# Second attention of a vision block: a gathering matmul for two units at once, and heads' rows stored dense on 68 partitions

## The reference, cut to what matters

```python
    def _L0_ffn_ref(x, Wq, bq, Wk, bk, Wv, bv, Wr, br, Wo, bo):
        ...
        dist = jax.nn.softmax(jnp.mean(x @ Wr + br, axis=1), axis=-1)
        _, idx = jax.lax.top_k(dist, N_ACTIVE)
        idx = jnp.sort(idx, axis=-1)
        ...
        Qs, Ks, Vs = (gather(Q), gather(K), gather(V))
        scale = 1.0 / jnp.sqrt(jnp.asarray(D_ATTN, x.dtype))
        score = jax.nn.softmax(jnp.einsum('bhqd,bhkd->bhqk', Qs, Ks) * scale, axis=-1)
        O = jnp.einsum('bhqk,bhkd->bhqd', score, Vs)
        O = O.transpose(0, 2, 1, 3).reshape(b, s, N_ACTIVE * D_ATTN)
        return O @ Wo + bo
    h = _L0_tok_ref(x, L0_tok_W, L0_tok_b, L0_tok_pos_emb)
    h = jnp.concatenate([jnp.broadcast_to(cls_tok, (h.shape[0], 1, h.shape[2])), h], axis=1)
    h = h + _L0_attn_ref(_layernorm(h, axis=-1), ...)
    h = h + _L0_ffn_ref(_layernorm(h, axis=-1), ...)
```

## Time and profile before

| what | value |
|---|---|
| device time, three runs | 388.31, 391.5, 392.24 us; median 391.5 |
| the profiled execution | 390.81 us, of which 389.0 us from its first to its last instruction (span) |
| busy share of the span | PE 81%, PEld 65%, DVE 66%, ACT 52%, POOL 44% |
| mean clock granted to PE | 0.851 of full |
| first weight transfer of the loop issued, last one issued | 224.8 us, 335.2 us |
| last stores of heads' rows issued | from 353.5 us |

### The profile page before, as it was taken

The page is one execution under the profiler, slowest core; times in us unless marked ns, Lnnn a source line. Parts: engine busy times, 40 slices in busy tenths (PEclk is TensorE's granted clock), DMA queues, the critical chain, the costliest instruction groups (busy, mean ns, idle before and its releaser), DMA issues.

```text
span 389.0 us, 14942 instructions
## 1 busy us (share of the span) xinstructions
PE 314.6 (81%) x6334; PEld 253.9 (65%) x6334; DVE 257.0 (66%) x546; ACT 203.2 (52%) x463; POOL 169.3 (44%) x193
## 2 busy tenths in 40 slices
PE   1999999888977888785897468998889698585787
PEld 0897768535855565554795258888789687483366
DVE  2355446455578888887696776797878678462365
ACT  1023323465877777742488037777777566352320
POOL 4755000004266666642055074576657656563200
PEclk9999999999975555555698559999999999679989
DMA  7997810003500000000000068999998899824714
GB/s 206 373 424 246 248 79 0 0 0 127 199 4 5 4 3 6 3 5 3 3 2 1 0 211 266 287 289 288 258 284 272 241 286 276 249 51 97 229 54 178
DMA packets 52275, 55.97 MB, mean 144 GB/s; under 512 B 25296, under 2 KB 49008, under 8 KB 51696
## 3 DMA queue, kind: packets, MB, share of 16 engines
q1 hardware_dynamic: 51632, 52.78, 43.1%
q0 software_dynamic: 576, 2.23, 1.8%
HBM read 45.04 MB, written 9.96 MB: 141 GB/s over the span
## 4 chain that ended last, share of the span: by engine, by line
PE 37%; SPq 23%; DVE 14%; issue 10%; DMA 6%; ACT 6%; POOL 4%; POOLq 0%; ACTq 0%; DVEq 0%
SPq L457 21%; PE ps L1366 11%; PE ps L1389 5%; PE ps L1520 4%; POOL r L527 4%; DVE r L1022 4%; PE ps L1727 3%; PE ps L1449 2%; DVE rs L1032 2%; PE ps L1404 2%; PE ps L1471 2%; DVE mx L1007 2%; DMA ring<-wsplit 2%; DMA r<-in_x 2%; DMA r<-padded_rows,idx 2%
## 5 line engine op out<-in xcount | busy, mean ns | idle before, releaser
L520 POOL TENSOR_TENSOR r<-r,cst 128x1088 f32<-128x1088 f32 x16 | 33.0, 2062 | 61.6 <-DVE ring L958 58.7
L1366 PE MATMUL ps<-r 128*128 128x256 f32 x192 | 45.8, 395 | 8.6 <-DMA r<-in_x 8.6
L1366 PEld LDWEIGHTS ps<-r 128*128 128x128 f32 x192 | 37.7, 199 | 15.6 <-issue 10.5
L805 ACT ACTIVATE r<-ps 128x504 f16<-128x504 f32 (+1 forms) x50 | 31.9, 664 | 27.9 <-PE ps L1571 27.5
L1594 PE MATMUL ps<-r,ring 128*128 128x68 f16 x840 | 34.6, 201 | 12.2 <-DMA ring<-wsplit 11.3
L1471 PE MATMUL ps<-r 17*32 17x34 f32 x2048 | 30.5, 242 | 16.1 <-DVE r L1022 11.2
L1471 PEld LDWEIGHTS ps<-r 17*32 17x32 f32 x2048 | 27.3, 142 | 24.1 <-DVE r L1022 18.3
L1594 PEld LDWEIGHTS ps<-r,ring 128*128 128x128 f16 x840 | 32.1, 101 | 16.5 <-DMA ring<-wsplit 13.2
L733 ACT ACTIVATE r<-r,cst 128x136 f32<-128x136 f32 x128 | 39.9, 401 | 0.0
L609 POOL TENSOR_TENSOR r<-r,quad 128x476 f16<-128x476 f16 x38 | 37.4, 1010 | 0.6
L527 POOL TENSOR_TENSOR r<-r,rinv 128x544 f32<-128x544 f32 x16 | 18.3, 1142 | 35.3 <-DVE rinv L1036 35.3
(11 more groups left out here) (170 smaller groups left out, 696.2 us busy)
## 6 DMA issues: line engine op xcount, KB each, us to landing
ring<-wsplit SPq DMA_DIRECT2D x140, 192.0 KB, 3.3
r<-in_x SPq DMA_DIRECT2D x3, 1536.0 KB, 15.9
padded_rows<-r SPq DMA_DIRECT2D x9, 448.0 KB, 5.2
r<-in_w SPq DMA_DIRECT2D x4, 768.0 KB, 7.5
wsplit<-ring SPq DMA_DIRECT2D x1, 3072.0 KB, 11.6
r<-in_x SPq DMA_DIRECT2D x4, 384.0 KB, 8.9
h<-in_pos SPq DMA_DIRECT2D x1, 1536.0 KB, 12.1
out<-h SPq DMA_DIRECT2D x3, 512.0 KB, 2.9
```

The source lines that it names most:

```text
L520: pool.tensor_tensor(free(kx[:, u % 2, 0, :], (ROWH, UI), (NTOK, HH), (1, NTOK)), free(kr[:, 0, UI * NTOK * u:], (NTOK, UI), (0, HH), (1, ...
L1366: mm = pe.matmul(bank((n - 1) % 2, 0, D), xT[:, c, k, i * P:(i + 1) * P], tokw[:, k, :], start=k == 0, stop=k == PKT - 1)
```

## The change

It does four things in the second attention.

1. A gathering matmul has 112 moving columns, for two units. xg becomes two buffers, each for a pair of units: `xg_even` at the old place and `xg_odd` in the allocation r1. A pair of units takes 17 fills of 4 matmuls: 16 of 4 tokens of one k, and one with the last token of all four k. 17 fills stand before unit 0; units 0 to 7 gather for the pair of units that comes two later, 9 fills in even and 8 in odd units; unit 8 gathers nothing.
2. The block-diagonal matrices have a pitch of 17 columns a pair, 68 in all, so weigh2 writes 68 partitions, and o2 is stored from 68 partitions, 14 pieces of 256 B each, dense, into `pair_rows`.
3. The values get a 65th column of ones (zeros in the low half), so weigh2 also gives the sum of the exponentials. `total` and `inverse` leave; `head_out` takes a reciprocal of 7 sums from the bank before each multiplication.
4. The pair table is made in three pieces: units 0 and 1, units 2 and 3 (behind the drains of the first 17 fills), the rest in unit 1.

```diff
-PITCH = QROW * HD2
+PITCH = NTOK * HD2
+VCOL = HD2 + 2
...
-            return bass.AP(padded_rows.tensor, (v * PU + IPG * lo) * PITCH, [(HD2, P), (IPG * PITCH, n), (1, HD2)])
+            return bass.AP(pair_rows.tensor, (v * PU + IPG * lo) * PITCH, [(HD2, TCOL), (IPG * PITCH, n), (1, HD2)])
...
-        NFILL = 8
-        FILL_ACT = [0, 2, 4, 6, 7]
-        FILL_DVE = [1, 3, 5]
...
+        NFILL = 17
+        SLOT_ON_ACT = (True, False, True, False, True, False, True, True)
+        EXTRA = 1
+        FILLS = []
+        for u in range(0, NV, 2):
+            FILLS += [(u, 2, (k,), first, 4) for k in range(2 * KT) for first in range(0, NTOK - 1, 4)]
+            FILLS += [(u, 2, tuple(range(2 * KT)), NTOK - 1, 1)]
+        ON_ACT = [at % 3 != 1 for at in range(NFILL)]
+        IN_SLOT = {}
+        for v in range(NV - 2):
+            for f, on_act in enumerate(SLOT_ON_ACT):
+                IN_SLOT[v, f] = [len(ON_ACT)]
+                ON_ACT.append(on_act)
+                if f == EXTRA and v % 2 == 0:
+                    IN_SLOT[v, f].append(len(ON_ACT))
+                    ON_ACT.append(True)
...
             def store_rows(v):
                 sp.wait_ge(o2_ready, 2 * (v + 1))
-                sp.dma_start(rows_of(v), o2[:, v % 2]).then_inc(o2_stored[v % 2], 16)
+                sp.dma_start(rows_of(v), o2[0:TCOL, v % 2]).then_inc(o2_stored[v % 2], 16)
...
-            for u in range(2):
-                pool.memset(free(bd[:, u, 0, 0, NTOK:], *gaps), 0.0).then_inc(bd_clear, 1)
+            for x in range(2):
+                pool.memset(free(v2[:, 0, x, 0, HD2:], (2 * GU * VCOL, 2), (VCOL, GU), (1, 1)), 1.0 - x).then_inc(ones_set, 1)
...
+                if v == 0:
+                    clear_odd_gaps(0)
+                    clear_odd_gaps(KT)
...
-                pool.indirect_dma_start(og[:, s, :], None, padded_rows,
+                pool.indirect_dma_start(og[:, s, :], None, pair_rows,
...
+            def head_out(v, r):
+                at = 2 * v + r
+                dve.wait_ge(pv2_done, at + 1)
...
+                dve.reciprocal(rinv[0:TCOL, r, 0:GR], free(bank(weigh_bank(v, r), HD2)[0:TCOL], (VCOL, GR)))\
+                    .then_inc(rinv2_ready, 1)
+                dve.wait_ge(rinv2_ready, at + 1)
+                dve.tensor_tensor(o2[0:TCOL, v % 2, GR * r:GR * r + GR, :],
+                                  free(bank(weigh_bank(v, r))[0:TCOL], (VCOL, GR), (1, HD2)),
+                                  free(rinv[0:TCOL, r, :], (1, GR), (0, HD2)), ALU.mult).then_inc(o2_ready, 1)
...
+            def gather_fill(at):
+                u, units, ks, first, tokens = FILLS[at]
+                if u in (2, 4) and begins_unit(at, ON_ACT[at]):
+                    pe.wait_ge(pairs_ready, u // 2 + 1)
...
+                cols = PU * units
+                for i, (k, n) in enumerate((k, first + n) for k in ks for n in range(tokens)):
                     x = (xh, xl)[k // KT]
                     lo = P * (k % KT)
-                    mm = pe.matmul(bank(fill_bank(at), PU * i, PU * i + PU), x[:, n, lo:lo + P],
-                                   pairs_of[:, PU * v:PU * v + PU], start=True, stop=True)
+                    mm = pe.matmul(bank(fill_bank(at), cols * i, cols * i + cols), x[:, n, lo:lo + P],
+                                   pairs_of[:, PU * u:PU * u + cols], start=True, stop=True)
...
-                        mm = pe.matmul(bank(weigh_bank(v, r), HD2 * i, HD2 * i + HD2), bd[:, v % 2, b, g, :], v2[:, v % 2, x, g, :],
-                                       start=m == 0, stop=m == 2)
+                        mm = pe.matmul(bank(weigh_bank(v, r), VCOL * i, VCOL * i + HD2 + 1)[0:TCOL], bd_of(v)[:, b, g, :],
+                                       v2[:, v % 2, x, g, 0:HD2 + 1], start=m == 0, stop=m == 2)
```

More of the change, by code:

```diff
@@ L218, in build @@
         bo_ready = sem("bo_ready")
[L219 removed]
+        ones_set = sem("ones_set")
         picked = sem("picked")
@@ L374, in build, with fills_until, filled_by, begins_unit @@
         OG_FIRST = 4
[L375 to L381 removed]
+        NFILL = 17
[14 more added lines that the diff above has]
+                    ON_ACT.append(True)
+        assert len(ON_ACT) == len(FILLS)
+        def fills_until(at, on_act):
+            return sum(e == on_act for e in ON_ACT[:at])
+        def filled_by(v):
+            return 1 + max(at for at, (u, n, *_) in enumerate(FILLS) if u <= v < u + n)
+        def begins_unit(at, on_act):
+            return at == min(i for i in range(len(FILLS)) if FILLS[i][0] == FILLS[at][0] and ON_ACT[i] == on_act)
+        def fill_ends(at):
+            u, units, ks, first, n = FILLS[at]
+            if len(ks) > 1:
+                return (free(xg_of(u)[:, 0, first:], (2 * PU * QROW, len(ks)), (QROW, PU * units)),
+                        free(bank(fill_bank(at)), (PU * units, len(ks)), (1, PU * units)))
+            return (free(xg_of(u)[:, ks[0], first:], (QROW, PU * units), (1, n)),
+                    free(bank(fill_bank(at)), (1, PU * units), (PU * units, n)))
         block = ctx.enter_context(nc.Block())
@@ L796, in _, with fill_out, fills_out @@
             act.wait_ge(wo1_done, NTOK)
-            def fill_out(v, f):
-                at = NFILL * v + f
+            def fill_out(at):
+                u = FILLS[at][0]
                 act.wait_ge(fill_done, at + 1)
-                if v >= 2 and f == 0:
-                    act.wait_ge(v2_in, 2 * (v - 1))
-                    act.wait_ge(qk_done, 2 * (v - 1))
-                first, n = fill_tokens(f)
-                nc.scalar.activation(free(xg[:, v % 2, f // 2, first:], (QROW, PU), (1, n)),
-                                     free(bank(fill_bank(at)), (1, PU), (PU, n)), ACT.Copy).then_inc(fill_act, 1)
+                if u >= 4 and begins_unit(at, True):
+                    act.wait_ge(v2_in, 2 * (u - 2))
+                    act.wait_ge(qk_done, 2 * (u - 2))
+                dst, src = fill_ends(at)
+                nc.scalar.activation(dst, src, ACT.Copy).then_inc(fill_act, 1)
+            def fills_out(v, *slots):
+                for f in slots:
+                    for at in IN_SLOT.get((v, f), ()):
+                        if ON_ACT[at]:
+                            fill_out(at)
             def q_out(v, r):
@@ L1185, in _, with fill_out, fills_out @@
             one_hot(0, 2 * PU)
-            def fill_out(v, f):
-                at = NFILL * v + f
+            def fill_out(at):
+                u = FILLS[at][0]
                 dve.wait_ge(fill_done, at + 1)
-                if v >= 2 and f == 1:
-                    dve.wait_ge(v2_in, 2 * (v - 1))
-                    dve.wait_ge(qk_done, 2 * (v - 1))
-                first, n = fill_tokens(f)
-                dve.tensor_copy(free(xg[:, v % 2, f // 2, first:], (QROW, PU), (1, n)),
-                                free(bank(fill_bank(at)), (1, PU), (PU, n))).then_inc(fill_dve, 1)
+                if u >= 4 and begins_unit(at, False):
+                    dve.wait_ge(v2_in, 2 * (u - 2))
+                    dve.wait_ge(qk_done, 2 * (u - 2))
+                dst, src = fill_ends(at)
+                dve.tensor_copy(dst, src).then_inc(fill_dve, 1)
+            def fills_out(v, *slots):
+                for f in slots:
+                    for at in IN_SLOT.get((v, f), ()):
+                        if not ON_ACT[at]:
+                            fill_out(at)
             def q_low(v, r):
```

161 lines of the change are left out of this document (76 added, 85 removed).

## The result

| | before | after |
|---|---|---|
| device time, median | 391.87 us (388.31 to 394.69) | 407.54 us (406.77 to 410.35) |
| ratio of times | | 1.042 (95%: 1.037 to 1.048) |
| profiled execution, its span | 390.81, 389.0 us | 407.63, 405.8 us |

What follows compares the result with a forecast made beforehand. The prediction took SP's stream of weight transfers to bound the kernel. Stores in the loop +11.4, tail stores +4.0 and reciprocals +0.5 sum to +15.9 us, giving 406.5 us, own range 399 to 412.

Steps and rivals of the forecast that it cites:

- What bounds: In the second attention's unit loop, SP's stream of weight transfers sets the pace; PE waits for weights.
- four engines: Each 68-row store goes to 4 DMA engines in equal shares of 17 rows, taking 4.25 us instead of 2.0.
- rival A: The 68 rows go to all 16 engines, 4 or 5 each, so the kernel takes 386 us; chance 0.20.
- the late start at zero: More fills before unit 0 start PE's qk(0,0) 5.5 us later, absorbed before SP needs the slots: zero, +1 at worst.
- The slack: Before the change, v_of(0,0) ends at 235.7 us and SP reaches its 22nd transfer, which needs the freed slots, about 239.6.
- the sign of being wrong altogether: In SP's waits, the projection of PE shows up as releaser.
- The store in the loop: Six stores ahead of the last weights cost the stream +1.9 us more each, +11.4 us in all (8 to 15).
- The two bounds of the prediction: Added stream time per store in the loop: at least +1.3 us (+2.25 less 1.0 idle), at most +2.5 us.
- The tail: The last stores, of units 7 to 9, end +4.0 us later (3 to 5); reciprocals before them add +0.5 us.
- Gathering, drains, reciprocals: Wider gathering matmuls and 85 drains of 0.6 to 0.75 us on ACT cost zero; reciprocals of 0.2 us add +0.5 us.
- Rival C: As forecast, but PE's clock falls too and PE sets the pace part of the time: about +10, 416 us; chance 0.12.
- The other signs: Transfers behind stores blocked about 4 us and more, store units near 13.9 us, DMA share some 0.78, quarter rate, later landings.

Runs made afterwards that it cites:

- e3: The kernel before, with only 68 of 128 rows of each store written (four engines), the result incomplete; 399.81 us, ratio 1.026 to the kernel before.
- e8: The kernel before, with only 72 of 128 rows of each store written (twelve engines), the result incomplete; 386.68 us, ratio 0.987 to the kernel before.
- e6: The changed kernel with the mended start of e5 and each store split into 64 and 4 rows; 391.60 us, ratio 1.003 to the kernel before.
- e1: The changed kernel with each store of 68 rows split into transfers of 64 and 4 rows; 395.46 us, ratio 1.011 to the kernel before.
- e9: The changed kernel with the mended start of e5 and the 80-row stores of e11; 387.64 us, ratio 0.987 to the kernel before.
- e11: The changed kernel with stores of 80 rows on 16 engines, gather indices adapted, five small DVE operations added; 393.37 us, ratio 1.004 to the kernel before.
- e5: The changed kernel, start mended: pair table for units 0 to 3 made first, odd-buffer clearing earlier, single-token fill drained on ACT; 402.59 us, ratio 1.027.
- e2: The changed kernel with the pair table for units 0 to 3 made in one piece before the fills; 407.22 us, ratio 1.040 to the kernel before.
- e10: The changed kernel with the mended start of e5, 68-row stores and tiles 128 rows apart in HBM; 401.99 us, ratio 1.022 to the kernel before.

## Why the prediction was right in its sum and wrong in its terms

That the sum came out within 1.1 us is luck: the mechanism of the store was right, but its size and the start were not.

- **What bounds, and four engines: right.** The stream of transfers set the pace, 68 rows went to four engines, and rival A is out. e3 and e8, four rows apart, differ by 3.9 points of the ratio.
- **The failed step: the late start at zero.** The prediction had PE's first unit 5.5 us later, set `v_of` at 239.5 against SP's arrival at 239.6, and called that a fit. There were three mistakes. PE was 7.3 us later, not 5.5, mostly because the drain of single tokens took 2.17 us. The 3.5 us from there to the end of v_of(0,0) held at full clock only: behind PE's pause of 3.5 us they were 5.6, and v_of(0,0) ended at 243.5. And I followed the late work only up to there: the third piece of the pair table, behind it on DVE, stopped PE once more for 2.9 us in unit 1, and SP waited another 3.3 us. The slack itself was read well (3.9 us against 3.4 and 3.5), but a margin of 0.1 us carried a term. What the start is worth in time lies between 3 us (e6 against e1) and 6 to 7 (e9 against e11); e5 has 6 by the ratios. Between the profiled executions of e5 and the changed kernel it is 3.8: 6.9 us at the first store, of which the costlier loop takes 4.0 back. The prediction had named SP's wait on the projection as the sign of being wrong altogether, and it was there. As a sign it went too far: this term fell, but the stream is still what binds afterwards.
- **The store in the loop: right in sign, too dear.** +11.4 forecast, +7.4 in the changed kernel, +7.2 in e3: 1.2 a store, below even the lower bound of 1.3. The mis-sized term is the duration of a piece. I took the 17.9 ns of the earlier trace rows, seen with 16 engines writing. Four engines alone move 72.5 GB/s, 18.1 each, so a piece of 256 B takes 14.1 ns and a store 238 x 14.1 = 3.36 us instead of 4.25. The two bounds of the prediction, redone with it, give (3.36 - 2.0) - 1.0 = +0.4 and 3.36 x 2.26 / 2.0 - 2.26 = +1.5; 1.2 lies between. It doesn't cover e5's 1.9.
- **The tail: +4.0 for the stores and 0.5 for the reciprocals forecast, +1.6 for both measured.** The chain that ended last, from the issue of unit 8's store on (start us, us, what), after:

```profile
366.21 5.05 DMA pair_rows<-r
371.26 4.21 issue
375.47 1.15 POOL r L701
376.62 0.30 POOLq L82
376.93 5.46 DMA r<-pair_rows,idx
```

and before:

```profile
350.89 3.78 DMA padded_rows<-r
354.67 3.55 issue
358.22 1.15 POOL r L647
```

POOL's first gather starts 9.3 us behind that issue, where it was 7.3, and 24.7 us behind the weights' end, where it was 22.6: 1.9 to 2.1 us more, and what follows the gather is 0.5 us shorter. The prediction's own sum for the tail, redone with 3.36 us a store for 4.25, has the last piece in at 352.0 + 3.36 + 3.36 = 358.7 instead of 360.5, which is +2.2 for +4.0. So the same piece time would do; that is an estimate, no run changes the tail alone.

- **Gathering, drains, reciprocals: as forecast.** In the groups by shape (count, busy us, mean ns, idle) a reciprocal takes 0.2 us, and the drains of ACT 659 ns, inside the forecast's 0.6 to 0.75, but as a mean of 0.54 for most and 2.16 for the single-token fills, which I had not priced apart. Eight gathering matmuls of 112 columns took 245.66 - 245.27 = 0.39 us by PE's timeline, 49 ns each, against 2 x 26.5 for two of 56: joining them saves PE little.

```profile
L859 ACT ACTIVATE r<-ps 128x448 f16<-128x448 f32 x55 | 34.9, 659 | 28.7 <-PE ps L1620 27.8
...
L1317 DVE RECIPROCAL rinv<-ps 68x7 f32<-68x7 f32 x20 | 3.9, 197 | 4.4 <-PE ps L1697 4.1
```

- **Rival C:** its sign, ring waits growing by less than 10 us, was met (18.1 against 11.3 us in the same view), but the sign was badly made: waits in the first units vanished into PE's own lateness. The clock's mean of 0.98 from 262 to 335 us speaks against it as a cause of the loop's length. Its 9.6 us of PE work in a unit of 13.7 us follow from no row either: the earlier trace rows give 61 / 73 x 12.0 = 10.0 us, and the forecast's own unit was 13.9.
- **The other signs:** a ring transfer behind a store blocked 2.7 to 3.9 us (4 and more forecast, 1.5 to 3.0 before); units with a store 13.1 us (13.9); DMA share 0.76 (0.78); a third, not a quarter, of the rate. All in the direction of four engines, all milder but the share. PE's step behind the last stores starts 374.77 - 368.85 = 5.9 us behind their issue, where it was 357.52 - 353.49 = 4.0: +1.9 for a forecast of about 4. The later landing can't be read, since the profile gives none for the new stores.

```profile
374.77 7.49 PE L1469 MATMUL ps<-ident 128*128 128x512 f16 x24 [6.14 <-DMA pair_rows<-r]
```

**Open:** why the loop costs 1.9 us a store in e5 (and e2 and e10) and 1.2 in e3 and the changed kernel. An early start seems partly given back while four-engine stores are in the stream; e10 excludes the addresses. The three costlier loops also have the lower mean clocks from first store to weights' end, 0.92 in e5 and 0.95 in e10 and e2, against 0.96 in the changed kernel and 0.97 in e3; whether that is a cause or a consequence no run shows. Of the three edits of e5 only the table was tried alone.

## What to carry to other kernels

Before cutting a transfer's rows, ask how many engines will share them, and count them in a trace, as above by the small packets. In this case 64, 80 and 128 rows went to 16 engines, 72 to 12 and 68 to 4, and with 80 rows stored for 68 the changed kernel took 393.37 us for 407.54 (e11): the padding was worth more than the bytes it added. Call a later start free only with a margin larger than the error of its estimate, and follow the late work through the next unit. And a sum that comes out right proves none of its terms: undo each one alone.

## What the runs showed of the hardware that I had not expected

- Four DMA engines that wrote 256 B pieces to HBM moved 18.1 GB/s each (72.5 in all in the changed kernel, 364 to 375 us), sixteen 13.6 each (218 in all). Whether sixteen meet a limit for all together isn't shown; twelve, in e8's last store, moved 178 to 218 GB/s in all (351.7 to 352.4 us).
- A DVE instruction of 336 elements a partition took 2.96 us beside POOL's memsets (the changed kernel; 2.95 and 2.96 in e1 and e2) and 0.39 us with POOL idle (e5, e6, e9, e10). In the kernel before one of 448 took 0.43 us at 231.03 us beside a memset of POOL, so not every such pair was slow.
- Draining 448 elements as single tokens, 2 bytes in every 64, took 2.16 to 2.19 us on ACT (all kernels with the gather for two units) and 2.17 to 2.20 on DVE (the changed kernel, e1, e2, e11), against 0.54 and 0.62 us for runs of four tokens.
- Storing 68 rows was 13 us (by medians) to 15 us (by ratios) dearer than 72 in this kernel, for eleven transfers (e3 against e8).
